# Attention block of a small audio tower: four maxima products a unit in place of six, in a new order

## Chip, cores and metric

The kernel runs on one core of one Trainium2 chip. The metric is the device time of one execution in microseconds (us). The kernel before takes 1871.29 us, the median of 3 runs from 1869.54 to 1872.24.

## What is computed

Three blocks run one after another over 128 batches: a tokenizer (4-token windows with a small softmax), attention, and a routed feed-forward block. Only the attention is touched. Per batch, of 128 rows and 192 features:

```python
# 8 heads of 24 features; thirds q3,q4,q5 / k3,k4,k5 / v3,v4,v5 of 8 features each
x3 = attn(q4, concat(k3, k4), concat(v3, v4))
x4 = attn(q5, concat(k3, k5), concat(v3, v5))
x5 = attn(q5, concat(k4, k5), concat(v4, v5))
h = h + concat(x3, x4, x5) @ w_proj.T + b_proj
```

`attn` is softmax(q k^T / sqrt(24)) v. Each query row's maximum over its keys is subtracted before the exponential, so every head needs the query-key products twice: once for the maxima, and once for the scores with the maximum folded in.

## The kernel before

**Stage and bodies.** `attend` (from L453) runs as a software pipeline, one batch a body. The loop holds four bodies a round, 30 rounds (bodies 3 to 122), and the bodies before and after are written out. Body i computes the scores of batch i, while other steps work on batches up to four ahead or three behind. A body has four units (u = 0 to 3) on TensorE; a unit has two heads a, b of batch i to score, and two heads c, d whose maxima it takes, of batch i + 1 for u = 0, 1 and of batch i + 2 for u = 2, 3. The four heads lie in four different row groups of 32 rows of the array, so products of different heads can run side by side, while two products of one head share rows.

**A unit on TensorE** (`products`, from L571). Six score products of 256 columns (L583) fill three PSUM banks: p_s1 with head b, p_s0 with head a, p_s5 with a and then b. Six maxima products (L587) fill p_maxa, which has two banks, and p_maxb, which has one. Where two row groups write one bank, the second waits on a semaphore that the first sets at its end: `pe_half` for p_s5 and `pe_fc` for p_maxa's second bank (blocks 4 and 5, 128 columns each from c and from d). Other waits at the unit's products: `dve_ma`, `dve_mb` (VectorE has read p_maxa, p_maxb of the unit before), `act_e1`, `act_e5`, `act_e0` (ScalarE has read the score banks). In unit 2 the first maxima product also waits for the transposes of the batch's keys and queries, `dma_k` and `dma_q`.

**Between the units** stand on TensorE: probabilities times values (L658, 24 products a body), the products of q, k, v of batch i + 3 right behind unit 2 (`qkv`, L627 to L633, into p_z), the transposes of the outputs (L669), and the projection right behind unit 3.

**The other engines.** ScalarE takes three exponentials a unit (L701, L704, L707), copies p_z to `raw` (L725) and `vn` (L726) once qkv is done, and `ot` (L716). VectorE reduces p_maxa (L749) and p_maxb (L751) in each unit; behind unit 1 it makes the minima of the negated maxima and writes them to `qk` (L766 to L768), and it has a few steps more (L757, L774, L777, L784). GpSimd splits `raw` into high and low halves: the keys at L802 and L805 (which sets `pool_k`), the queries at L808 and L811 (`pool_q`), L813 (`pool_q5`); and it does so for x and for the attention's output.

**The SP queue** issues five DMA transposes a body, in this order: xt (L535), kt (L540, waits for `pool_k`), qt (L545, waits for `pool_q`, `pe_ma[1]`, `pe_mb[1]`), yt (L550), qm (L556, waits for `dve_min`, `pool_q5`, `pe_s0[3]`). Keys and queries that body i transposes are of batch i + 2, and so unit 2 of the same body is their first user. Each wait is `ready`: a wait and an increment, with the count computed from the loop's register where it isn't one that a register holds already.

Of the kernel before, what the change touches and what calls it, by code (L numbers as in the profile page):

```python
# [15 lines left out]
NP = 127  # L16
# [434 lines left out]
def attend(nc, t, NB):  # L451

    with ExitStack() as ctx:  # L453
# [69 lines left out]
        def _(sp):  # L523

            def ready(signal, count):

                sp.wait_ge(signal, count)
                sp.sem_inc(sp_ready, 1)

            def body(i, r):  # L530
# [5 lines left out]
                if within(i + 2, NB):  # L536
                    ready(pool_k, seen(i + 3))
                    if within(i - 2, NB):
                        ready(pe_s0[3], seen(i - 1))
                    sp.dma_start_transpose(kt[:, (r + 2) % U].rearrange("p k g n -> p (k g) n"), qk[:, r % 2, K0:K0 + 768]).then_inc(dma_k, 16)  # L540
                    ready(pool_q, seen(i + 3))
                    if within(i, NB):
                        ready(pe_ma[1], seen(i + 1))
                        ready(pe_mb[1], seen(i + 1))
                    sp.dma_start_transpose(qt[:, r % 2].rearrange("p k g n -> p (k g) n"), qk[:, r % 2, 0:512]).then_inc(dma_q, 16)  # L545
# [24 lines left out]
        def _(pe):  # L570
# [3 lines left out]
            def products(i, r, u):  # L574
# [15 lines left out]
                if has_s:  # L590
                    if u == 0:
                        pe.wait_ge(dma_qm, seen(16 * (i + 1)))
                    pe.wait_ge(act_e1[u - 1] if u else act_e1[3], seen(i + 1 if u else i))
                    score(p_s[1][:, 0:2, :], b, 0, slice(0, 2))
                if has_m:
                    if u == 2:
                        pe.wait_ge(dma_k, seen(16 * (bm + 1)))
                        pe.wait_ge(dma_q, seen(16 * (bm + 1)))
                    pe.wait_ge(dve_ma[u - 1], seen(i + 2 if u < 3 else i + 3))
                    maximum(p_ma[:, 4:5, :], c, 1, slice(2, 3)).then_inc(pe_fc[u], 1)  # L600
# [3 lines left out]
                if has_m:  # L604
                    maximum(p_ma[:, 0:2, :], d, 0, slice(0, 2))
                if has_s:
                    score(p_s[1][:, 2:4, :], b, 1, slice(0, 3, 2)).then_inc(pe_s1[u], 1)
                if has_m:
                    maximum(p_ma[:, 2:4, :], d, 1, slice(0, 2))
                    pe.wait_ge(pe_fc[u], seen(bm + 1))  # L610
                    maximum(p_ma[:, 5:6, :], d, 1, slice(2, 3)).then_inc(pe_ma[u], 1)
                    pe.wait_ge(dve_mb[u - 1], seen(i + 2 if u < 3 else i + 3))
                    maximum(p_mb[:, 0:2, :], c, 0, slice(0, 2))
# [3 lines left out]
                if has_m:  # L617
                    maximum(p_mb[:, 2:4, :], c, 1, slice(0, 2)).then_inc(pe_mb[u], 1)
                if has_s:
                    pe.wait_ge(pe_half[u], seen(2 * i + 1))  # L620
                    score(p_s5[:, 2:4, :], b, 2, slice(1, 3)).then_inc(pe_half[u], 1)
                    score(p_s[0][:, 2:4, :], a, 1, slice(0, 3, 2)).then_inc(pe_s0[u], 1)
# [110 lines left out]
        def _(dve):  # L733
# [10 lines left out]
            def maxima(i, r, u):  # L744
                bm, pair = (i + 1, 2 + (1 - u)) if u < 2 else (i + 2, 1 - (u - 2))
                q = (r + 1) % 2 if u < 2 else r % 2
                if within(bm, NB):
                    dve.wait_ge(pe_ma[u], seen(bm + 1))
                    nc.vector.tensor_reduce(top[:, q, pair, 4:10], p_ma[:, 0:6, 0:NP], AX.X, ALU.max, negate=True).then_inc(dve_ma[u], 1)  # L749
# [3 lines left out]
            def body(i, r):  # L753
# [6 lines left out]
                if within(i + 1, NB):  # L760
                    dve.wait_ge(dve_mb[1], seen(i + 2))
                    got = top[:, (r + 1) % 2]
                    four = got[:, :, 0:8].rearrange("p a (e k) -> p a e k", e=2)
                    fifth = got[:, :, 8:10]
                    low = [slots((r + 1) % 2, 256 * x, HEADS)[:, :, 24].rearrange("p (a e) -> p a e", e=2) for x in range(3)]
                    nc.vector.tensor_tensor(low[0], four[:, :, :, 0], four[:, :, :, 1], ALU.min)  # L766
                    nc.vector.tensor_tensor(low[1], four[:, :, :, 2], fifth, ALU.min)
                    nc.vector.tensor_tensor(low[2], four[:, :, :, 3], fifth, ALU.min).then_inc(dve_min, 1)  # L768
# [442 lines left out]
```

## Time and profile before

| | |
|---|---|
| median of 3 runs | 1871.29 us |
| profiled execution, its own time | 1873.42 us |
| its span in the profile | 1871.7 us |
| tokenizer, about | 0 to 320 us of the span |
| attention | about 370 to 1400 us |
| feed-forward, about | 1450 to 1871 us |
| TensorE busy, whole span | 1789.6 us, 96% |
| VectorE, ScalarE, GpSimd busy | 1495.4, 1462.8, 1252.7 us |

The profile is of one execution. Busy times are sums of the instructions' spans; on TensorE products overlap and their ends are modelled, so that a busy TensorE need not be at its peak. Of a row group's work only starts can be compared exactly.

### The profile page before, as it was taken

Reading aid. Unit: us, or ns where it says so; the run is one execution under the profiler, and the core shown is the slowest. Engines: PE = TensorE matmul, PEld = TensorE weight load, DVE = VectorE, ACT = ScalarE, POOL = GpSimd, SP = SyncE. Lnnn points to the kernel's source line nnn. Section 1 sums busy time; section 2 is a strip of 40 time slices with the busy share of each in tenths; the row PEclk is TensorE's granted clock in tenths of the full one; section 3 lists DMA queues with packets and bytes.
Section 4 is the critical chain, followed back from the end, with each engine's and each line's share of the span. In section 5 each row is a group of like instructions: output and inputs, shape, how many; then the busy total and the mean of one; then the engine's idle time right before and its main releaser. Section 6 shows DMA issues by size and latency. Waiting matters only on the chain. (4 is left out here: it accounts for less than half of the span.)

```text
span 1871.7 us, 59000 instructions
## 1 busy us (share of the span) xinstructions
PE 1789.6 (96%) x20032; PEld 1015.8 (54%) x20032; DVE 1495.4 (80%) x3674; ACT 1462.8 (78%) x2983; POOL 1252.7 (67%) x2306
## 2 busy tenths in 40 slices
PE   5999999599999999999999999999994999999999
PEld 3677777244444444444444444444442777777776
DVE  6887878689999999999999999999994555555554
ACT  4666666288889888988898889988884777777775
POOL 4777776467777777777777777777753565666661
PEclk9999999699999999999999999999997999999999
DMA  7344442144444444444444444444441333333332
GB/s 192 90 112 112 112 112 68 35 81 87 89 88 89 89 88 88 90 88 90 88 88 88 90 89 89 87 92 88 88 79 28 72 70 68 70 67 71 65 74 54
DMA packets 503935, 159.49 MB, mean 85 GB/s; under 512 B 452176, under 2 KB 503120, under 8 KB 503888
## 3 DMA queue, kind: packets, MB, share of 16 engines
q1 hardware_dynamic: 503888, 158.90, 40.0%
q8 instruction: 26, 0.43, 0.1%
q14 instruction: 21, 0.17, 0.0%
HBM read 37.26 MB, written 12.48 MB: 27 GB/s over the span
## 5 line engine op out<-in xcount | busy, mean ns | idle before, releaser
L749 DVE TENSOR_REDUCE tops<-p_maxa 128x6 f32<-128x762 f32 x512 | 482.4, 942 | 63.2 <-PE p_maxa L587 61.4
L658 PE MATMUL p_o<-probs,vn 127*32 127x256 f32 x6144 | 410.8, 385 | 0.3 <-DVE att L777 0.3
L583 PE MATMUL p_s<-qm,kt 32*128 32x256 f16 x3072 | 399.9, 276 | 1.0 <-ACT probs L704 0.4
L701 ACT ACTIVATE probs<-p_s 128x512 f32<-128x512 f32 x512 | 305.4, 596 | 108.9 <-PE p_s L583 95.1
L751 DVE TENSOR_REDUCE tops<-p_maxb 128x4 f32<-128x508 f32 x512 | 345.9, 676 | 0.0
L707 ACT ACTIVATE probs<-p_s 128x512 f32<-128x512 f32 x512 | 309.0, 603 | 0.0
L704 ACT ACTIVATE probs<-p_s 128x512 f32<-128x512 f32 x512 | 304.6, 595 | 0.3 <-PE p_s L583 0.2
L587 PE MATMUL p_maxa<-kt,qt 24*128 24x256 f16 (+1 forms) x2048 | 283.9, 250 | 17.4 <-DMA qt<-qk 8.8
L1056 DVE TENSOR_TENSOR gel_lo<-gel,gel_hi 128x512 f16<-128x512 f32 x192 | 151.0, 787 | 168.9 <-ACT gel_hi L1028 168.7
L802 POOL TENSOR_TENSOR qk<-raw,one 128x384 f16<-128x384 f32 x128 | 105.7, 826 | 220.8 <-ACT raw L725 220.8
L583 PEld LDWEIGHTS p_s<-qm,kt 32*128 32x128 f16 x3072 | 135.2, 91 | 182.6 <-issue 164.8
L658 PEld LDWEIGHTS p_o<-probs,vn 127*32 127x32 f32 x6144 | 160.6, 109 | 131.4 <-issue 48.8
L1020 ACT ACTIVATE gel<-f_w,b 128x512 f32<-128x512 f32 x192 | 131.9, 687 | 117.4 <-PE f_w L969 117.3
L587 PE MATMUL p_maxb<-kt,qt 24*128 24x256 f16 x1024 | 200.5, 275 | 0.1
L980 PE MATMUL f_y<-w_hi,gel_hi 128*128 128x192 f16 x768 | 188.8, 246 | 0.2 <-DVE gel_lo L1056 0.2
L982 PE MATMUL f_y<-w_hi,gel_lo 128*128 128x192 f16 x768 | 188.9, 246 | 0.0
L981 PE MATMUL f_y<-w_lo,gel_hi 128*128 128x192 f16 x768 | 188.9, 246 | 0.0
L1126 POOL TENSOR_TENSOR f_hx<-f_hn,f_one 128x192 f16<-128x192 f32 x120 | 85.3, 711 | 154.0 <-ACT f_hn L1007 146.9
L587 PEld LDWEIGHTS p_maxa<-kt,qt 24*128 24x128 f16 x2048 | 109.1, 91 | 139.9 <-PE p_maxa L587 108.0
L208 ACT ACTIVATE tanhs<-pa 128x384 f32<-128x384 f32 x128 | 62.7, 490 | 99.8 <-PE pa L154 99.8
L1028 ACT ACTIVATE gel_hi<-gel 128x512 f16<-128x512 f32 x192 | 120.9, 630 | 7.1
L396 POOL TENSOR_TENSOR diag<-ident,weight 128x256 f32<-128x256 f32 x128 | 79.2, 620 | 54.2 <-DVE weight L296 45.0
(213 smaller groups left out, 4556.9 us busy)
## 6 DMA issues: line engine op xcount, KB each, us to landing
xt_a<-in_xt SPq DMA_DIRECT2D x32, 512.0 KB, 4.4
xt_b<-in_xt SPq DMA_DIRECT2D x64, 256.0 KB, 5.2
out<-out_sb SPq DMA_DIRECT2D x32, 336.0 KB, 2.6
xt<-hx SPq DMA_TRANSPOSE x128, 2.4
kt<-qk SPq DMA_TRANSPOSE x128, 2.8
qt<-qk SPq DMA_TRANSPOSE x128, 2.4
qm<-qk SPq DMA_TRANSPOSE x128, 2.7
yt<-ay SPq DMA_TRANSPOSE x128, 2.3
```

Of the source, the lines that this page charges most:

```text
L583: return nc.tensor.matmul(o, kt[full(j), r, kind, g, :], qm[full(j), r % 2, versions, g, :], start=True, stop=True, skip_group_check=True)
L587: return nc.tensor.matmul(o, qt[short(j), rq, kind, gm, :], kt[short(j), rk, cols, gm, :], start=True, stop=True, skip_group_check=True)
L658: last = nc.tensor.matmul(p_o[32 * j:32 * j + 32, blocks, :], vn[0:NP, r, src:src + 32], probs[0:NP, r % 2, QUAD * g + j, kind * 256:(kind ...
L701: nc.scalar.activation(probs[:, r % 2, h + 1, 0:512], p_s[1][:, :, :].rearrange("p x n -> p (x n)"), ACT.Exp, scale=SCALE).then_inc(act_e1 ...
L704: nc.scalar.activation(probs[:, r % 2, h:h + 2, 512:768], p_s5[:, :, :].rearrange("p (h x) n -> p h (x n)", h=2), ACT.Exp, scale=SCALE).th ...
L707: nc.scalar.activation(probs[:, r % 2, h, 0:512], p_s[0][:, :, :].rearrange("p x n -> p (x n)"), ACT.Exp, scale=SCALE).then_inc(act_e0[u], 1)
L749: nc.vector.tensor_reduce(top[:, q, pair, 4:10], p_ma[:, 0:6, 0:NP], AX.X, ALU.max, negate=True).then_inc(dve_ma[u], 1)
L751: nc.vector.tensor_reduce(top[:, q, pair, 0:4], p_mb[:, :, 0:NP], AX.X, ALU.max, negate=True).then_inc(dve_mb[u], 1)
L980: nc.tensor.matmul(o, ghi[:, c % 3, n], t.w2_hi[:, c, :], start=False, stop=False)
L981: nc.tensor.matmul(o, ghi[:, c % 3, n], t.w2_lo[:, c, :], start=False, stop=False)
L982: last = nc.tensor.matmul(o, glo[:, c % 3, n], t.w2_hi[:, c, :], start=False, stop=(c == HCH - 1))
L1056: nc.vector.tensor_tensor(glo[:, c % 3, :], gel[:, c % 2, :], ghi[:, c % 3, :], ALU.subtract).then_inc(dve_lo[c], 1)
```

## The change

The maxima of block k5 and of k3, k4 against q5 (kind 1) now come from one product of 384 columns for each of the heads c and d, each into a bank of p_maxa of its own. The two products of kind 0 share p_maxb, c first, d behind a wait on `pe_fc` at the unit's end. `pe_ma` counts to two a unit, so that its waiters (SP before qt, VectorE before the first reduction) wait for 2(n + 1) in place of n + 1. The reduction of p_maxa reads 2 x 3 blocks of 127, as many elements as before, and two minima instructions stand for three.

```diff
@@ SP queue, between kt and qt
                     if within(i, NB):
-                        ready(pe_ma[1], seen(i + 1))
+                        ready(pe_ma[1], seen(2 * (i + 1)))
                         ready(pe_mb[1], seen(i + 1))
@@ products(i, r, u)
                 if has_m:
-                    if u == 2:
-                        pe.wait_ge(dma_k, seen(16 * (bm + 1)))
-                        pe.wait_ge(dma_q, seen(16 * (bm + 1)))
                     pe.wait_ge(dve_ma[u - 1], seen(i + 2 if u < 3 else i + 3))
-                    maximum(p_ma[:, 4:5, :], c, 1, slice(2, 3)).then_inc(pe_fc[u], 1)
+                    maximum(p_ma[:, 0:3, :], c, 1, slice(0, 3)).then_inc(pe_ma[u], 1)
+                    maximum(p_ma[:, 4:7, :], d, 1, slice(0, 3)).then_inc(pe_ma[u], 1)
                 if has_s:
                     pe.wait_ge(act_e5[u - 1] if u else act_e5[3], seen(i + 1 if u else i))
                     score(p_s5[:, 0:2, :], a, 2, slice(1, 3)).then_inc(pe_half[u], 1)
-                if has_m:
-                    maximum(p_ma[:, 0:2, :], d, 0, slice(0, 2))
                 if has_s:
                     score(p_s[1][:, 2:4, :], b, 1, slice(0, 3, 2)).then_inc(pe_s1[u], 1)
                 if has_m:
-                    maximum(p_ma[:, 2:4, :], d, 1, slice(0, 2))
-                    pe.wait_ge(pe_fc[u], seen(bm + 1))
-                    maximum(p_ma[:, 5:6, :], d, 1, slice(2, 3)).then_inc(pe_ma[u], 1)
                     pe.wait_ge(dve_mb[u - 1], seen(i + 2 if u < 3 else i + 3))
-                    maximum(p_mb[:, 0:2, :], c, 0, slice(0, 2))
+                    maximum(p_mb[:, 0:2, :], c, 0, slice(0, 2)).then_inc(pe_fc[u], 1)
                 if has_s:
                     pe.wait_ge(act_e0[u - 1] if u else act_e0[3], seen(i + 1 if u else i))
                     score(p_s[0][:, 0:2, :], a, 0, slice(0, 2))
-                if has_m:
-                    maximum(p_mb[:, 2:4, :], c, 1, slice(0, 2)).then_inc(pe_mb[u], 1)
+                    score(p_s[0][:, 2:4, :], a, 1, slice(0, 3, 2)).then_inc(pe_s0[u], 1)
                 if has_s:
                     pe.wait_ge(pe_half[u], seen(2 * i + 1))
                     score(p_s5[:, 2:4, :], b, 2, slice(1, 3)).then_inc(pe_half[u], 1)
-                    score(p_s[0][:, 2:4, :], a, 1, slice(0, 3, 2)).then_inc(pe_s0[u], 1)
+                if has_m:
+                    pe.wait_ge(pe_fc[u], seen(bm + 1))
+                    maximum(p_mb[:, 2:4, :], d, 0, slice(0, 2)).then_inc(pe_mb[u], 1)
@@ VectorE, body
-                    nc.vector.tensor_tensor(low[0], four[:, :, :, 0], four[:, :, :, 1], ALU.min)
-                    nc.vector.tensor_tensor(low[1], four[:, :, :, 2], fifth, ALU.min)
-                    nc.vector.tensor_tensor(low[2], four[:, :, :, 3], fifth, ALU.min).then_inc(dve_min, 1)
+                    nc.vector.tensor_tensor(low[:, 0], fourth[:, :, :, 0], fourth[:, :, :, 1], ALU.min)
+                    nc.vector.tensor_tensor(low[:, 1:3], fifth[:, 0:2], fifth[:, 2:3].broadcast_to([128, 2, QUAD, 2]), ALU.min).then_inc(dve_min, 1)
```

The waits on `dma_k` and `dma_q` are still taken in unit 2 in front of the first maxima product.

TensorE, unit 2 of the loop's third body, before (p_s1, p_s5, p_s0 are score banks; what stands behind the unit is qkv):

```order
L583 MATMUL p_s1<-qm,kt 128x256 [waits act_e11]
L587 MATMUL p_maxa<-kt,qt 128x128 [waits dve_ma1,dma_q,dma_k]
L583 MATMUL p_s5<-qm,kt 128x256 [waits act_e51]
L587 MATMUL p_maxa<-kt,qt 128x256
L583 MATMUL p_s1<-qm,kt 128x256
L587 MATMUL p_maxa<-kt,qt 128x256
L587 MATMUL p_maxa<-kt,qt 128x128 [waits pe_fc2]
L587 MATMUL p_maxb<-kt,qt 128x256 [waits dve_mb1]
L583 MATMUL p_s0<-qm,kt 128x256 [waits act_e01]
L587 MATMUL p_maxb<-kt,qt 128x256
L583 MATMUL p_s5<-qm,kt 128x256 [waits pe_half2]
L583 MATMUL p_s0<-qm,kt 128x256
```

The same unit of the changed kernel:

```order
L583 MATMUL p_s1<-qm,kt 128x256 [waits act_e11]
L587 MATMUL p_maxa<-kt,qt 128x384 [waits dve_ma1,dma_q,dma_k]
L587 MATMUL p_maxa<-kt,qt 128x384
L583 MATMUL p_s5<-qm,kt 128x256 [waits act_e51]
L583 MATMUL p_s1<-qm,kt 128x256
L587 MATMUL p_maxb<-kt,qt 128x256 [waits dve_mb1]
L583 MATMUL p_s0<-qm,kt 128x256 [waits act_e01]
L583 MATMUL p_s0<-qm,kt 128x256
L583 MATMUL p_s5<-qm,kt 128x256 [waits pe_half2]
L587 MATMUL p_maxb<-kt,qt 128x256 [waits pe_fc2]
```

The wait on `pe_fc` stood at the seventh of twelve products and stands at the last of ten; the product that it waits for was the second of the unit, of 128 columns, and is now the sixth, of 256.

The SP queue in the loop's second body, as a difference (the third and fourth body change alike):

```order
 L535 DMA_TRANSPOSE xt<-hx 128x3x128 [waits pool_x,pe_qkv]
 L540 DMA_TRANSPOSE kt<-qk 128x6x128 [waits pool_k,pe_s03]
-L545 DMA_TRANSPOSE qt<-qk 128x4x128 [waits pool_q,pe_ma1,pe_mb1]
+L527 REGISTER_ALU [waits pool_q]
+L545 DMA_TRANSPOSE qt<-qk 128x4x128 [waits pe_ma1,pe_mb1]
 L550 DMA_TRANSPOSE yt<-ay 128x3x128 [waits pool_y,pe_proj]
```

The new count needs a register instruction between kt and qt. The loop's first body had one there before the change, and has now an instruction that updates several registers in its place.

## Rows read from the trace of the kernel before

**Rows 1.** Busy times by stretch; PEclk is the granted share of TensorE's clock:

```profile
400.00:1400.00 1000.00, 995.54 (x13509) 459.12 (x13505) 934.28 (x1841) 895.65 (x1840) 730.16 (x1456) 1.00 0.45 88
```

**Rows 2.** Who waited for whom, 600 to 1300 us (86 bodies): us, times, longest:

```profile
POOL qk L802 <- ACT raw L725: 138.9, 87, 1.9
...
PEld p_maxa L587 <- PE p_maxa L587: 73.2, 346, 0.2
```

**Rows 3.** Timeline, unit 2 of a second body: start us, duration us, engine, line:

```profile
800.36 0.21 PE L587 MATMUL p_maxa<-kt,qt 24*128 24x128 f16 x1
...
800.37 0.28 PE L587 MATMUL p_maxa<-kt,qt 24*128 24x256 f16 x1
...
800.49 0.37 PE L587 MATMUL p_maxa<-kt,qt 24*128 24x256 f16 x2
...
800.63 0.09 PEld L587 LDWEIGHTS p_maxa<-kt,qt 24*128 24x128 f16 x1 [0.15 <-PE p_maxa L587]
...
800.70 0.10 PEld L583 LDWEIGHTS p_s<-qm,kt 32*128 32x128 f16 x2
...
800.76 0.27 PE L583 MATMUL p_s<-qm,kt 32*128 32x256 f16 x1
...
800.96 0.39 PE L627 MATMUL p_z<-wqkv_ahi,xt 128*128 128x512 f16 x1
```

**Rows 4.** Timeline, from that unit's products to unit 2 one body on:

```profile
802.25 0.44 ACT L725 ACTIVATE raw<-p_z 128x320 f32<-128x320 f32 x1
...
803.66 0.55 POOL L805 TENSOR_TENSOR qk<-raw,qk 128x192 f16<-128x192 f32 x1
...
804.38 1.21 SPq L540 DMA_TRANSPOSE kt<-qk  x1
...
805.84 1.19 SPq L545 DMA_TRANSPOSE qt<-qk  x1
...
808.28 0.28 PE L583 MATMUL p_s<-qm,kt 32*128 32x256 f16 x1
808.33 0.21 PE L587 MATMUL p_maxa<-kt,qt 24*128 24x128 f16 x1
...
808.99 0.39 PE L627 MATMUL p_z<-wqkv_ahi,xt 128*128 128x512 f16 x1
```

**Rows 5.** Timeline of the SP queue, a fourth body's end and a first body:

```profile
813.88 1.19 SPq L545 DMA_TRANSPOSE qt<-qk  x1
...
819.19 1.19 SPq L535 DMA_TRANSPOSE xt<-hx  x1
820.63 1.21 SPq L540 DMA_TRANSPOSE kt<-qk  x1
822.15 1.19 SPq L545 DMA_TRANSPOSE qt<-qk  x1
```

**Rows 6.** Timeline of TensorE, unit 2 of a fourth and of a first body:

```profile
816.39 0.21 PE L587 MATMUL p_maxa<-kt,qt 24*128 24x128 f16 x1
...
817.02 0.39 PE L627 MATMUL p_z<-wqkv_ahi,xt 128*128 128x512 f16 x1
...
824.65 0.21 PE L587 MATMUL p_maxa<-kt,qt 24*128 24x128 f16 x1
```

**Rows 7.** Groups by line and shape, 600 to 1300 us: count, busy us, mean ns:

```profile
L587 PE MATMUL p_maxb<-kt,qt 24*128 24x256 f16 x691 | 133.9, 273 | 0.0
```

**Rows 8.** Timeline, weight load and product of unit 0 in the body between:

```profile
804.75 0.23 PE L587 MATMUL p_maxa<-kt,qt 24*128 24x128 f16 x1
...
805.09 0.09 PEld L587 LDWEIGHTS p_maxa<-kt,qt 24*128 24x128 f16 x1 [0.23 <-PE p_maxa L587]
```

**Rows 9.** Timeline of VectorE, unit 0 and the last of the minima there:

```profile
805.35 0.95 DVE L749 TENSOR_REDUCE tops<-p_maxa 128x6 f32<-128x762 f32 x1 [0.36 <-PE p_maxa L587]
...
809.18 0.18 DVE L768 TENSOR_TENSOR qk<-tops 128x8 f16<-128x8 f32 x1
```

**Rows 10.** Timeline of GpSimd in that first body:

```profile
819.73 0.55 POOL L805 TENSOR_TENSOR qk<-raw,qk 128x192 f16<-128x192 f32 x1
```

More of the change, by code:

```diff
@@ L594, in products @@
                     score(p_s[1][:, 0:2, :], b, 0, slice(0, 2))
+                if has_m and u == 2:
+                    pe.wait_ge(dma_k, seen(16 * (bm + 1)))
+                    pe.wait_ge(dma_q, seen(16 * (bm + 1)))
                 if has_m:
-                    if u == 2:
-                        pe.wait_ge(dma_k, seen(16 * (bm + 1)))
-                        pe.wait_ge(dma_q, seen(16 * (bm + 1)))
                     pe.wait_ge(dve_ma[u - 1], seen(i + 2 if u < 3 else i + 3))
-                    maximum(p_ma[:, 4:5, :], c, 1, slice(2, 3)).then_inc(pe_fc[u], 1)
+                    maximum(p_ma[:, 0:3, :], c, 1, slice(0, 3)).then_inc(pe_ma[u], 1)
+                    maximum(p_ma[:, 4:7, :], d, 1, slice(0, 3)).then_inc(pe_ma[u], 1)
                 if has_s:
@@ L747, in maxima @@
                 if within(bm, NB):
-                    dve.wait_ge(pe_ma[u], seen(bm + 1))
-                    nc.vector.tensor_reduce(top[:, q, pair, 4:10], p_ma[:, 0:6, 0:NP], AX.X, ALU.max, negate=True).then_inc(dve_ma[u], 1)
+                    dve.wait_ge(pe_ma[u], seen(2 * (bm + 1)))
+                    nc.vector.tensor_reduce(top[:, q, pair, 4:10].rearrange("p (e k) -> p e k", e=2),
+                                            p_ma[:, :, :].rearrange("p (e k) n -> p e k n", e=2)[:, :, 0:3, 0:NP],
+                                            AX.X, ALU.max, negate=True).then_inc(dve_ma[u], 1)
                     dve.wait_ge(pe_mb[u], seen(bm + 1))
@@ L762, in body @@
                     got = top[:, (r + 1) % 2]
-                    four = got[:, :, 0:8].rearrange("p a (e k) -> p a e k", e=2)
-                    fifth = got[:, :, 8:10]
-                    low = [slots((r + 1) % 2, 256 * x, HEADS)[:, :, 24].rearrange("p (a e) -> p a e", e=2) for x in range(3)]
-                    nc.vector.tensor_tensor(low[0], four[:, :, :, 0], four[:, :, :, 1], ALU.min)
-                    nc.vector.tensor_tensor(low[1], four[:, :, :, 2], fifth, ALU.min)
-                    nc.vector.tensor_tensor(low[2], four[:, :, :, 3], fifth, ALU.min).then_inc(dve_min, 1)
+                    fourth = got[:, :, 0:4].rearrange("p a (e k) -> p a e k", e=2)
+                    fifth = got[:, :, 4:10].rearrange("p a (e k) -> p k a e", e=2)
+                    low = slots((r + 1) % 2, 0, NQ)[:, :, 24].rearrange("p (x a e) -> p x a e", x=3, e=2)
+                    nc.vector.tensor_tensor(low[:, 0], fourth[:, :, :, 0], fourth[:, :, :, 1], ALU.min)
+                    nc.vector.tensor_tensor(low[:, 1:3], fifth[:, 0:2], fifth[:, 2:3].broadcast_to([128, 2, QUAD, 2]), ALU.min).then_inc(dve_min, 1)
                 maxima(i, r, 2)
```

## Prediction

> **What bounds the kernel now.** I read the busy times by stretch first. From 400 to 1400 us TensorE is busy for 995.54 of 1000 us, VectorE for 934.28, ScalarE for 895.65, and the granted clock is 1.00, the 2.4 GHz level [rows 1]. So TensorE looks like the bound, and two products fewer a unit look like a gain. But its spans overlap, so this share cannot tell whether a unit may end sooner. The waits add two things: GpSimd's L802 waits for ScalarE's `raw` in every body, and TensorE waits 0.21 us (73.2 over 346) for a product of its own in every unit, which is the wait on `pe_fc` [rows 2].
>
> The timeline then shows a loop through five engines that closes once a body:
> - Unit 2's first maxima product starts at 800.36, qkv at 800.96: 0.60 us [rows 3].
> - `raw` starts at 802.25: 1.29 us after qkv. L805, which sets `pool_k`, ends at 804.21, kt is issued at 804.38, qt at 805.84 [rows 4].
> - The next unit 2's first maxima product starts at 808.33, 2.49 us after qt [rows 4]. In the fourth body it is 2.51 us (813.88 to 816.39), in the next first body 2.50 us (822.15 to 824.65) [rows 5, 6].
>
> The last is the sign: behind the issue of qt this product comes at the same distance in every body, whenever the unit began. In the body of 808.28 the unit's first score product is only 0.05 us ahead [rows 4], so TensorE's own work is just covered there. The kernel is bound by the latency of this loop, with TensorE close behind. From the second body's product (800.36) to the fourth's (816.39) are two turns, 8.02 us each; to the next first body's (824.65) it is 8.26 us. On the mean a body lasts 8.1 us (691 p_maxb products, 8 a body, in 700 us [rows 7]).
>
> **Unit 2, from its first maxima product to qkv.** Before, this is 0.60 us in the second body (and in the first, which waits for qt alike), 0.66 in the third (808.33 to 808.99) and 0.63 in the fourth (816.39 to 817.02) [rows 3, 4, 6]. After the change a chain of three links decides it, since the unit's last product waits for the sixth:
> - Two products of one head follow each other at 0.12 us if the first has 256 columns (800.37 to 800.49) [rows 3]. A 128-column product lasts 0.23 us in unit 0 [rows 8] and a 256-column one 0.28 [rows 3], so 128 columns more are 0.05 us: 384 columns take 0.17 us, and then c's p_maxb product can start.
> - Its end must be seen. No row has this for a maxima product of 256 columns. The nearest two: from 128 columns at 800.36 to the load that waits for them at 800.63, 0.27 us; from the score product of 256 columns on p_s5, issued with the maxima at 800.36, to the load that waits for it at 800.70, 0.34 us [rows 3]. The second has the same columns, and the first plus 0.05 us gives nearly it, so I take 0.34. The low end is 0.27. The high end is 0.39: in unit 0 the 128-column product starts at 804.75 and the load that waits for it at 805.09, 0.34 us [rows 8], and 0.05 us for the columns come on top.
> - From a unit's last product to what follows: 0.20 us (800.76 to 800.96) [rows 3].
>
> Sum: 0.17 + 0.34 + 0.20 = 0.71 us. That is 0.11, 0.05, 0.08 and 0.11 us more in the second, third, fourth and first body: **+0.35 us a round** of four. Of this VectorE takes no share: its first reduction waits 0.36 us for TensorE in unit 0 [rows 9], and both 384-column products are done some 0.2 us sooner than the last p_maxa product was. So p_maxb is free for unit 2 earlier than before.
>
> Here the Trainium skill has a rule that speaks for the change. It says that each matmul carries about 60 cycles of overhead on trn2, whatever its columns ("TensorEngine Tiling (Array Packing)", Instruction Overhead). By it two products fewer would take some 0.05 us off a unit at 2.4 GHz, my estimate from its figure, and unit 2 would come to 0.66 us. The trace does not bear it out on this path: products of different heads start within 0.01 us of each other (800.36 and 800.37) [rows 3].
>
> **The SP queue.** Between kt and qt a register instruction is added in the second, third and fourth body. The first body had one before, and there kt to qt is 1.52 us (820.63 to 822.15) [rows 5] against 1.46 (804.38 to 805.84) [rows 4]. I take 0.07 us: three times that is **+0.21 us a round**. The first body's own exchange I cost at nothing; its bounds are 0 and 0.03. Nothing hides this term, since qt's issue is a link of the loop. The ends are 0 and 0.10 for each body.
>
> **The minima and what they release.** VectorE's work in units 0 and 1 moves ahead by about 0.2 us, and one of the minima goes. So `dve_min` comes 0.3 us or more sooner (the last of the minima ended at 809.36 [rows 9]), qm and xt are issued sooner, and the queue is free earlier for kt. This pays only where kt waits for the queue and not for GpSimd. In the second body L805 ends at 804.21 and kt comes 0.17 us later [rows 4]. In the first body L805 ends at 820.28 and kt comes 0.35 us later, at 820.63, with xt just ahead of it (819.19 plus 1.44) [rows 5, 10]. Of this 0.35 the usual 0.17 and 0.07 for the register instruction stay: **-0.11 us a round**. Bounds: 0, and -0.18.
>
> **Units 0, 1 and 3** are off the loop. They come to 0.71 us by the same three links where they were 0.67, and unit 1, which waits for VectorE, gets a little shorter. Cover for this is the wait for qt, which grows to 0.1 to 0.3 us in every body because the loop gets longer than TensorE's own work. If that cover is gone, three units by 0.04 us come on top, 0.1 us a body. The new waits of VectorE on two counts cost nothing, as the second product starts with the first. Tokenizer and feed-forward are untouched.
>
> **Sum.** 0.35 + 0.21 - 0.11 = 0.45 us a round, times 30 rounds = 13.5 us. Some 8 bodies outside the loop have no register instructions: 0.09 us each, 0.7 us. Together +14.2 us. Against the profiled execution's own 1873.42 us this gives 1887.6. The median of the runs lies 2.1 us lower, so the forecast is **1885.5 us**.
>
> **Rivals.**
> 1. *The completion wait is covered* and unit 2 gets shorter: if c's p_maxb product is over when the others are done, unit 2 takes 0.17 + 0.12 + 0.20 = 0.49 us, 0.53 us a round less than before in place of 0.35 more. With SP's +0.21 and -0.11 it is -0.43 a round: 1858 us. It decides when the wait costs under about 0.23 us. For it: the wait has moved from the middle of the unit to its end. Against it: only three score products stand between, and the two measured waits are 0.27 and 0.34. Chance 0.07. In this case the kernel is faster.
> 2. *The number of products decides.* If TensorE's own work were the bound and each product had a cost of its own in it, 8 fewer a body would show. Two products in a row on one row group stand 0.12 us apart, where 256 columns at 2.4 GHz take 0.107: 0.013 us each, times 8 and 128 is 13 us, 1858 us. For it: TensorE's 99.6%. Against it: the constant 2.50 us behind qt. By the overhead rule of the Trainium skill ("TensorEngine Tiling (Array Packing)", Instruction Overhead) it would be 26 us, an estimate. Chance 0.03.
> 3. *Unit 2 stays as long as it was*, since the first part of the wait is absorbed, and only SP's terms are left: +0.10 us a round, 3 us, 1874.3 us. This takes a wait of 0.25 us, close to the 128-column row. Chance 0.10.
> 4. *TensorE's own work becomes the bound*, if the three links cost more in units 0, 1 and 3 than worked out, say 0.80 in place of 0.71 us in each unit: 0.09 by four is 0.36 us a body, of which about 0.2 is covered. 0.16 by 126 is 20 us on top: about 1905 us. Chance 0.05.
>
> **Numbers.** The forecast's case has 0.75. Its own range, from the bounds: with 0.27 for the wait in all four bodies it is 8.4 us less, 1877; with 0.39 for the wait and 0.10 for each of SP's instructions it is 8.7 us more, 1894. The full range has to hold 8 in 10 and reaches from 1873, which takes in rival 3, to 1896. Two measurements of this kernel can tell 0.2% (3.7 us) from no change. Faster: rivals 1 and 2, 0.10. Same: most of rival 3, 0.10. Slower: 0.80.
>
> **What the profile after would show.** Unit 2 from its first maxima product to qkv: 0.71 us in all four bodies. Its first maxima product still 2.50 us behind qt's issue, and at least 0.1 us behind the unit's first score product in every body. kt to qt 1.52 or 1.53 us in all four bodies. kt in the first body 0.24 us behind L805's end. VectorE's idle time before L746 smaller in unit 0, and TensorE's wait for its own product kept, now at the load for p_maxb. A body of 8.22 us. I am wrong if unit 2 takes under 0.65 us, or if the distance from qt's issue to the first maxima product varies.

## The result, and the profile after

The changed kernel takes 1893.81 us (median of 4 runs, 1891.67 to 1896.09), the kernel before 1870.41 us beside it (1869.08 to 1872.24): a ratio of 1.0125, 95% interval 1.0107 to 1.0142. It is slower by 23.4 us, where 14.2 us were forecast. The profiled execution took 1896.09 us, with a span of 1894.4 us.

Busy times of the changed kernel in the same stretch as [rows 1]; the columns are TensorE, weight loads, VectorE, ScalarE, GpSimd, then the granted clock:

```profile
400.00:1400.00 1000.00, 997.49 (x12255) 511.24 (x12256) 905.70 (x1682) 875.25 (x1803) 720.08 (x1440) 1.00 0.44 87
```

TensorE's share rose from 99.6% to 99.7%, the clock is still at its 2.4 GHz level, and VectorE, ScalarE and GpSimd are all less busy: their work is spread over longer bodies. The weight loads alone show more, 511.24 us for 459.12, though there are 1249 fewer of them; fewer of them overlap. Next the waits from 600 to 1300 us, against [rows 2]:

```profile
POOL qk L800 <- ACT raw L722: 153.3, 85, 2.0
...
PEld p_s L583 <- PE p_s L583: 51.9, 233, 0.2
...
PEld p_maxb L587 <- DVE tops L750: 13.2, 84, 0.2
```

GpSimd waits for `raw` 1.80 us a body, where it was 1.60. TensorE's wait for a product of its own moved, but not to where I put it: it is not the load for p_maxb but a load for p_s, the one that waits for `pe_half`. The last row, 0.16 us a body, is unit 1's wait for VectorE. The groups of the same stretch (count, busy us, mean ns), against [rows 7]:

```profile
L587 PE MATMUL p_maxb<-kt,qt 24*128 24x256 f16 x677 | 185.2, 274 | 0.0
L587 PE MATMUL p_maxa<-kt,qt 24*128 24x384 f16 x676 | 113.4, 330 | 0.0
```

677 products at 8 a body are 84.6 bodies in 700 us, 8.27 us each; before there were 86.4, 8.10 us each. The 384-column product lasts 0.33 us by the profile's modelled ends, 0.056 more than one of 256 columns (0.05 was estimated).

The timeline of unit 2 in a second body (start us, us; compare [rows 3]):

```profile
808.13 0.34 PE L587 MATMUL p_maxa<-kt,qt 24*128 24x384 f16 x2
808.14 0.10 PEld L583 LDWEIGHTS p_s<-qm,kt 32*128 32x128 f16 x2
808.14 0.39 PE L583 MATMUL p_s<-qm,kt 32*128 32x256 f16 x3
...
808.29 0.27 PE L587 MATMUL p_maxb<-kt,qt 24*128 24x256 f16 x1
...
808.58 0.09 PEld L583 LDWEIGHTS p_s<-qm,kt 32*128 32x128 f16 x1 [0.22 <-PE p_s L583]
808.64 0.09 PEld L587 LDWEIGHTS p_maxb<-kt,qt 24*128 24x128 f16 x1
...
808.86 0.39 PE L624 MATMUL p_z<-wqkv_ahi,xt 128*128 128x512 f16 x1
```

From the first maxima product to qkv it is now 0.73 us (0.60 before). a's p_s5 product starts with the 384-column ones at 808.14, and b's load, which waits for it, comes at 808.58: 0.44 us, where the same wait took 0.34 in [rows 3]. The unit's last product, d's on p_maxb, follows that load by 0.06 us.

The loop, from that unit on (compare [rows 4]):

```profile
810.15 0.44 ACT L722 ACTIVATE raw<-p_z 128x320 f32<-128x320 f32 x1
...
811.57 0.55 POOL L803 TENSOR_TENSOR qk<-raw,qk 128x192 f16<-128x192 f32 x1
812.28 1.22 SPq L540 DMA_TRANSPOSE kt<-qk  x1
813.83 1.19 SPq L545 DMA_TRANSPOSE qt<-qk  x1
...
816.28 0.28 PE L583 MATMUL p_s<-qm,kt 32*128 32x256 f16 x1
816.33 0.34 PE L587 MATMUL p_maxa<-kt,qt 24*128 24x384 f16 x2
...
817.05 0.39 PE L624 MATMUL p_z<-wqkv_ahi,xt 128*128 128x512 f16 x1
```

And the SP queue in the fourth and the first body that follow (compare [rows 5]):

```profile
820.48 1.21 SPq L540 DMA_TRANSPOSE kt<-qk  x1
822.07 1.19 SPq L545 DMA_TRANSPOSE qt<-qk  x1
...
828.79 1.21 SPq L540 DMA_TRANSPOSE kt<-qk  x1
830.36 1.19 SPq L545 DMA_TRANSPOSE qt<-qk  x1
```

The 2.50 us from qt to the first maxima product stand as before (813.83 to 816.33). kt to qt is 1.55, 1.59 and 1.57 us here, where it was 1.46 and, in the first body, 1.52.

**The loop added up.** All links taken singly over 600 to 1300 us, mean of a body in us. "kt late" runs from the end of GpSimd's second k operation (L805, now L803) to kt's issue, "unit 2" from its first maxima product to qkv. The links left out are raw to GpSimd's second k operation (1.44, up to 1.46 in e11), that operation itself (0.55) and qkv to raw (1.31). "Cover" is how far the first maxima product stands behind the unit's first score product: where it is 0.00 to 0.01 in a body, TensorE's own work holds that body.

| version | kt late | kt to qt | qt to unit 2 | unit 2 | cover | body | x126, against before | measured, ratio |
|---|---|---|---|---|---|---|---|---|
| before | 0.207 | 1.477 | 2.507 | 0.622 | 0.167 | 8.113 | | |
| the change | 0.180 | 1.558 | 2.508 | 0.728 | 0.132 | 8.276 | +20.5 | 1.0125 |
| e1_sp_count | 0.180 | 1.478 | 2.518 | 0.734 | 0.064 | 8.213 | +12.6 | 1.0083 |
| e2_before_count2 | 0.180 | 1.556 | 2.508 | 0.598 | 0.220 | 8.142 | +3.7 | 1.0019 |
| e3_p5_first | 0.179 | 1.568 | 2.505 | 0.697 | 0.150 | 8.253 | +17.6 | 1.0100 |
| e8_p5_first_count | 0.179 | 1.478 | 2.512 | 0.705 | 0.072 | 8.175 | +7.8 | 1.0066 |
| e4_repeat_unit2 | 0.180 | 1.559 | 2.507 | 0.835 | 0.131 | 8.381 | +33.8 | 1.0198 |
| e5_repeat_unit0 | 0.228 | 1.558 | 2.506 | 0.746 | 0.144 | 8.342 | +28.9 | 1.0166 |
| e10_after_unit2_only | 0.234 | 1.477 | 2.508 | 0.793 | 0.203 | 8.318 | +25.8 | 1.0130 |
| e9_after_units013 | 0.178 | 1.558 | 2.506 | 0.604 | 0.135 | 8.155 | +5.3 | 1.0035 |
| e11_after_unit1_only | 0.179 | 1.477 | 2.579 | 0.664 | 0.008 | 8.220 | +13.5 | 1.0048 |
| e12_mixed | 0.179 | 1.478 | 2.517 | 0.633 | 0.068 | 8.120 | +0.9 | 1.0017 |

The links add up to the body, to within 0.002 us for the kernel before and the change. Times 126, the bodies give the measured differences to within 5 us (e8: 7.8 by the bodies, 12.4 by the ratio; e11: 13.5 and 9.0). So the change's 23.4 us are, a round of four bodies: unit 2 +0.42, kt to qt +0.32, kt late -0.11, the rest +0.02, together 0.65 us, or 20.5 us over 126 bodies. The other 3 us come at the stage's end: in the profiled execution the last qkv but two starts 19.3 us later than before (1388.01 against 1368.75), the last one 23.4 us later (1408.97 against 1385.58). So the last two bodies take 10.0 and 11.0 us here, where e4, the change with one product more, has 9.0 and 8.5. No run tells the cause. One kt and one qt there took 2.62 and 1.76 us of the queue, where they take 1.2 elsewhere:

```profile
1391.44 2.62 SPq L540 DMA_TRANSPOSE kt<-qk  x1
1394.31 1.76 SPq L545 DMA_TRANSPOSE qt<-qk  x1
```

### The profile page after: what moved, and what is told of

Same layout as the page of the kernel before. It is cut to its first block and busy times, and to the rows that moved or that the text cites. A ratio compares the mean times of both kernels' runs of the same rounds, so it can differ in the third digit from the quotient of the medians.

```text
span 1894.4 us, 56914 instructions
## 1 busy us (share of the span) xinstructions
PE 1812.3 (96%) x19008; PEld 1078.8 (57%) x19008; DVE 1487.7 (79%) x3546; ACT 1460.4 (77%) x2983; POOL 1251.4 (66%) x2306
## 5 line engine op out<-in xcount | busy, mean ns | idle before, releaser
L583 PEld LDWEIGHTS p_s<-qm,kt 32*128 32x128 f16 x3072 | 164.7, 92 | 268.5 <-issue 177.8
L587 PE MATMUL p_maxb<-kt,qt 24*128 24x256 f16 x1024 | 282.9, 276 | 0.8
L655 PEld LDWEIGHTS p_o<-probs,vn 127*32 127x32 f32 x6144 | 160.6, 109 | 117.1 <-issue 20.5
L587 PE MATMUL p_maxa<-kt,qt 24*128 24x384 f16 x1024 | 173.6, 333 | 16.9 <-DMA qt<-qk 9.2
L587 PEld LDWEIGHTS p_maxb<-kt,qt 24*128 24x128 f16 x1024 | 93.5, 91 | 33.5 <-DVE tops L750 21.7
```

The lines of the kernel that those rows point to most:

```text
L583: return nc.tensor.matmul(o, kt[full(j), r, kind, g, :], qm[full(j), r % 2, versions, g, :], start=True, stop=True, skip_group_check=True)
L587: return nc.tensor.matmul(o, qt[short(j), rq, kind, gm, :], kt[short(j), rk, cols, gm, :], start=True, stop=True, skip_group_check=True)
L655: last = nc.tensor.matmul(p_o[32 * j:32 * j + 32, blocks, :], vn[0:NP, r, src:src + 32], probs[0:NP, r % 2, QUAD * g + j, kind * 256:(kind ...
```

## The experiments

Each was timed in five rounds against the kernel before.

**1. SP waits for VectorE's count.** Since VectorE reads p_maxa only when both products have been counted, its `dve_ma[1]` stands for both, and needs no doubled value.

```diff
-ready(pe_ma[1], seen(2 * (i + 1)))
+ready(dve_ma[1], seen(i + 1))
```

> The changed kernel, with SP's wait on two increments of pe_ma[1] ahead of qt replaced by a wait on dve_ma[1] for i + 1 (VectorE has read that bank), a count that a register holds already. Theory L (the loop raw, pool_k, kt, qt, unit 2, qkv bounds the body): kt to qt falls from 1.54 to 1.59 us back to 1.46 in three bodies of a round and to 1.53 in the first, 0.3 us a round, 8 to 10 us in all: 1884 to 1886 us. Theory P (TensorE's own work bounds the changed kernel): SP's queue costs nothing, 1893 to 1895 us.

Measured: 1887.84 us, ratio 1.0083 [1.0070, 1.0097], 6 us off the change by the medians and 8 by the ratios; theory P had nothing, theory L 8 to 10. Its SP queue in a fourth and a first body:

```profile
816.22 1.22 SPq L540 DMA_TRANSPOSE kt<-qk  x1
817.68 1.19 SPq L545 DMA_TRANSPOSE qt<-qk  x1
...
824.44 1.21 SPq L540 DMA_TRANSPOSE kt<-qk  x1
825.97 1.19 SPq L545 DMA_TRANSPOSE qt<-qk  x1
```

1.46 and 1.53 us are back. The register work between the two transposes is a link of the loop and cost 0.08 us a body in the mean, where the prediction's 0.21 us a round are 0.05: 0.07 or 0.08 in the second and third body, 0.13 in the fourth, 0.04 in the first. Not all of the 10 us came back: the cover is 0.003 us in the third and fourth body, so that TensorE's own work holds these two, with 2.53 us from qt to unit 2.

**2. The doubled count put into the kernel before.**

```diff
-ready(pe_ma[1], seen(i + 1))
+ready(pe_ma[1], seen(2 * (i + 1)))
...
-                    maximum(p_ma[:, 2:4, :], d, 1, slice(0, 2))
+                    maximum(p_ma[:, 2:4, :], d, 1, slice(0, 2)).then_inc(pe_ma[u], 1)
...
-                    dve.wait_ge(pe_ma[u], seen(bm + 1))
+                    dve.wait_ge(pe_ma[u], seen(2 * (bm + 1)))
```

> The kernel before with nothing changed but the count: pe_ma is also incremented by the product of blocks 2 and 3, so SP and VectorE wait for 2(n + 1). All products, their order and the minima stay. Theory L: kt to qt grows by 0.07 to 0.13 us in three bodies of a round, 0.2 to 0.33 us a round: 1876 to 1880 us. Theory P: 1870 to 1871 us, as before.

Measured: 1875.63 us, ratio 1.0019 [1.0009, 1.0028]. kt to qt grew by the same 0.079 us, 10 us over the kernel, but 6 of them came back. Two links shrank: kt late in the first body from 0.335 to 0.227, and unit 2 in the third and fourth body from 0.65 and 0.64 to 0.598, most likely since VectorE, which reads p_maxb of unit 1, had more time. So a delay at one link of this loop was not paid in full, because other links had been waiting for something outside it.

**3. One product repeated, in unit 2 and in unit 0.** The unit's last product is issued twice (the second version has `u == 0`).

```diff
+                    if u == 2:
+                        maximum(p_mb[:, 2:4, :], d, 0, slice(0, 2))
                     maximum(p_mb[:, 2:4, :], d, 0, slice(0, 2)).then_inc(pe_mb[u], 1)
```

> The changed kernel with the last product of unit 2 (d, kind 0, 256 columns) issued twice in a row, 0.12 us more of TensorE's work between the first maxima product and qkv. Theory L: the whole 0.12 us lies on the loop, 127 bodies, +15 us: 1908 to 1910 us. Theory P: +15 us too. The pair with the next run tells them apart.

> The changed kernel with the last product of unit 0 issued twice, the same 0.12 us of TensorE's work off the loop. Theory L: it is taken up by the wait for qt in unit 2, which was 0.13, 0.21, 0.05 and 0.12 us in the four bodies of a round; only the third body exceeds it, by 0.07 us a round: 1895 to 1898 us. Theory P: +15 us, 1908 to 1910 us.

Measured: unit 2 1.0198 [1.0184, 1.0212], 13.7 us over the change by the ratios; unit 0 1.0166 [1.0152, 1.0180], 7.7 us over it. The first is what the loop says: unit 2 is longer by 0.107 us a body, and all of it counts. By itself it can't tell the two theories apart, which both had 15 us for it. The second is not: unit 0 was to be covered (1895 to 1898 us were expected, 1903.25 measured), and more than half of its 0.11 us came through, although unit 1 took 0.07 us less behind it (0.740 for 0.812, as VectorE has read p_maxb by the time that the later unit needs it). The links tell how. The cover falls to 0.015 us in the third body, VectorE's reductions come later, and so do the minima, qm and xt on SP: kt late in the first body grows from 0.226 to 0.414 us. Unit 2 itself waits for VectorE in the third and fourth body (0.798 and 0.738). Units 0, 1 and 3 are off the loop, but not free. Nor does this pair tell the two theories apart: the four units together are 0.054 us a body longer than in the change, which is 6.8 us by theory P as well.

**4. a's p_s5 product ahead of the 384-column ones.**

```diff
+                if has_s:
+                    pe.wait_ge(act_e5[u - 1] if u else act_e5[3], seen(i + 1 if u else i))
+                    score(p_s5[:, 0:2, :], a, 2, slice(1, 3)).then_inc(pe_half[u], 1)
                 if has_m and u == 2:
...
                     maximum(p_ma[:, 4:7, :], d, 1, slice(0, 3)).then_inc(pe_ma[u], 1)
-                if has_s:
-                    pe.wait_ge(act_e5[u - 1] if u else act_e5[3], seen(i + 1 if u else i))
-                    score(p_s5[:, 0:2, :], a, 2, slice(1, 3)).then_inc(pe_half[u], 1)
```

> The change, with one thing moved: in each unit the score product of head a on p_s5 is issued ahead of the two 384-column maxima products and no longer behind them. In the changed kernel the load for b's product on p_s5, which waits for that product of a, comes 0.45 us behind its start, where the same wait took 0.34 us in the kernel before; the unit's last product comes 0.07 us behind it. Theory O (a product's completion is told in the order of issue, so 256 columns behind two products of 384 are told with these): the distance falls to 0.34 or 0.35 us, and the last product then waits for c's p_maxb product (0.18 + 0.34 = 0.51 us behind the first maxima product, where it was 0.53). A unit gets some 0.02 us shorter, and where the wait came from the score product even 0.05: 0.08 to 0.2 us a round in unit 2, so 2 to 6 us off 1893.8, 1888 to 1892. Rival D (the distance is 0.45 us because the product shares the array with three others, in whatever order they are issued): it stays 0.43 to 0.45 us, and the time within 0.1% of the change's.

> The same, and SP waits for VectorE's count in place of TensorE's doubled one, which takes the register instruction between kt and qt away in three of four bodies. That alone took 6 to 8 us off the change. If both links lie on the loop they add up: 1881 to 1886. If TensorE's own work is already the bound in the version with the other count (its bodies showed under 0.07 us between a unit's first score product and its first maxima product), only what the shorter units give counts: four units by 0.02 us are 0.08 us a body, 10 us, so 1877 to 1880. If neither counts any more, 1887 or 1888.

Measured: 1888.13 us, 1.0100 [1.0084, 1.0115], and with the other count 1881.24 us, 1.0066 [1.0052, 1.0079]. Unit 2 of the first of them:

```profile
812.12 0.34 PE L587 MATMUL p_maxa<-kt,qt 24*128 24x384 f16 x2
...
812.28 0.27 PE L587 MATMUL p_maxb<-kt,qt 24*128 24x256 f16 x1
...
812.60 0.28 PE L587 MATMUL p_maxb<-kt,qt 24*128 24x256 f16 x1
812.81 0.39 PE L624 MATMUL p_z<-wqkv_ahi,xt 128*128 128x512 f16 x1
```

In unit 0 b's p_s5 product came 0.346 us behind the unit's start, where it was 0.463, and the last product at 0.507, as theory O had it. In this kernel a product of 256 columns that is issued behind two of 384 is told with them, and rival D falls: beside the same other products the wait is 0.11 us shorter. Of the medians the move takes 5.7 us off the change, SP's count 6.0, both together 12.6: they add up, as links of one loop do. The last product now waits for c's p_maxb (812.28 to 812.60, 0.32 us): this is the chain that the prediction had, and it gives 0.69 us.

**5. qkv ahead of unit 2.** This opens the loop and leaves the work as it is. On ScalarE `raw` and `vn` stand between the two `exponentials` lines below. The diff is of the first version; in the second the removed count is `seen(i + 1)`.

```diff
+                    if within(i + 1, NB):
+                        ready(pe_mb[2], seen(i + 2))
...
-                    if within(i, NB):
-                        ready(pe_ma[1], seen(2 * (i + 1)))
-                        ready(pe_mb[1], seen(i + 1))
...
+                qkv(i)
                 products(i, r, 2)
-                qkv(i)
...
-                exponentials(i, r, 2)
...
+                exponentials(i, r, 2)
```

> The change, with qkv issued ahead of unit 2's products and not behind them, ScalarE's raw and vn copies ahead of unit 2's exponentials, and SP's waits between kt and qt replaced by one ahead of kt that has long been met. This opens the loop: raw no longer stands behind the landing of qt. Theory L (the loop is the bound and TensorE's own work close behind, about 8.16 us a body by the version with SP's other count): the body falls from 8.27 to 8.15 to 8.18 us and the time to 1878 to 1883; GpSimd's k pass no longer waits 0.26 us in the mean for raw. Rival T (TensorE's own work already sets 8.27 us): the time stays within 0.2% of 1893.8. Rival S: units 2 and 3 now follow each other without a pause, and ScalarE, with its two copies ahead of unit 2's exponentials, becomes late for p_s: TensorE's waits for L727 and its neighbours grow by over 0.1 us a body and the time goes over 1895.

> The same three moves in the kernel before. Theory L: the loop sets 8.11 us a body there, TensorE's own work 8.03 to 8.06 us (its first maxima product was 0.05 us behind the unit's first score product at the least); opened, the time falls from 1870.4 by 6 to 10 us, to 1860 to 1865. Rival T: TensorE's own work is the bound before as well, and nothing is gained: 1868 to 1872. Rival S: ScalarE is late in units 2 and 3, over 1875.

Measured: 1970.07 us, 1.0536 [1.0522, 1.0551], and 1971.02 us, 1.0531 [1.0516, 1.0545]. Both theories failed here: L had 1878 to 1883 and 1860 to 1865, T no change. It is rival S, and far larger than it was put. A body takes 8.95 to 8.97 us in both, whatever the products. Units 2 and 3 in the first of them:

```profile
801.49 0.44 ACT L720 ACTIVATE raw<-p_z 128x320 f32<-128x320 f32 x1 [0.66 <-PE p_z L629]
...
802.68 0.09 PEld L582 LDWEIGHTS p_s<-qm,kt 32*128 32x128 f16 x1 [0.26 <-ACT probs L697]
...
803.17 0.09 PEld L582 LDWEIGHTS p_s<-qm,kt 32*128 32x128 f16 x2 [0.29 <-ACT probs L700]
...
803.66 0.11 PEld L582 LDWEIGHTS p_s<-qm,kt 32*128 32x128 f16 x3 [0.19 <-ACT probs L703]
```

ScalarE waits 0.66 us for qkv, then unit 3 waits three times for ScalarE, 0.74 us together. In the kernel's own order qkv stands between units 2 and 3 and gives ScalarE that time. So what opens the loop costs more than the loop, and these two runs don't tell what the loop's removal alone would give.

**6. The change taken apart by unit.** In the first version unit 2 alone has the four products, in the second all units but 2, in the third unit 1 alone; the others issue the six products of before (the expectations say five by mistake). All three have the change's minima. SP waits as before in the first, for the doubled count in the second, for VectorE's count in the third. Maxima then land in other places of `tops` than the minima read, so the stabilizers are other ones.

```diff
+                if u == 2:
...
+                        maximum(p_ma[:, 4:5, :], c, 1, slice(2, 3)).then_inc(pe_fc[u], 1)
...
+                else:
...
-                    dve.wait_ge(pe_ma[u], seen(2 * (bm + 1)))
+                    if u == 2:
+                        dve.wait_ge(pe_ma[u], seen(bm + 1))
+                        nc.vector.tensor_reduce(top[:, q, pair, 4:10], p_ma[:, 0:6, 0:NP], AX.X, ALU.max, negate=True).then_inc(dve_ma[u], 1)
```

The condition shown is that of the second version; it is `u != 2` in the first and `u != 1` in the third.

> The kernel before, with the change's four products in unit 2 alone; units 0, 1 and 3 issue the five products of before, SP waits as before, the minima are the change's. (The maxima land in other places of tops than the minima read, so the stabilizers are wrong; the amount of work is the same.) Theory L (the loop through qt bounds the kernel): from its first maxima product to qkv unit 2 takes 0.72 or 0.73 us in place of 0.60 to 0.66, 0.41 us a round, less 0.08 to 0.11 for the first body, in which kt comes sooner: +9 to +11 us on 1870.4, so 1879 to 1882. Rival P (TensorE's own work bounds it): unit 2 is longer by 0.069 us a body in the mean, times 126 is 8.7 us, 1879; and the version with the other three units must then show more than this one.

> The change, with the five products of before in unit 2 alone; units 0, 1 and 3, the minima and SP's doubled count are the change's. (Stabilizers wrong, as in the version above.) Theory L: the loop has before's unit 2 and SP's term, 0.33 us a round less what the first body gives back, 3.5 to 7 us on 1870.4; TensorE's own work is longer by 0.068 - 0.046 + 0.070 = 0.09 us a body in these three units, where 0.05 us a body covers it: 1874 to 1878. Rival P: all of the 0.09 us counts, 11.6 us, 1882, and this version is slower than the one with the change in unit 2.

> The kernel before, with the change's four products in unit 1 alone (the one unit that they made shorter, 0.81 for 0.86 us), the minima of the change, and SP waiting for VectorE's count. (Stabilizers wrong again.) Theory L: unit 1 is off the loop, so its 0.05 us a body gives nothing; what is left is the first body's kt, up to 0.11 us a round, 0 to 3 us: 1867 to 1871. Rival P: 0.046 times 126 is 6 us more, 1861 to 1865, a kernel faster than before.

Measured: e10 1.0130 [1.0112, 1.0147], e9 1.0035 [1.0025, 1.0045], e11 1.0048 [1.0035, 1.0061]. Unit 2 alone carries as much as the whole change, the other units and SP's count together 6.5 us, so the parts do not add up to the whole. The order of the two is theory L's. But e10 came out at 24 us, not 9 to 11, and e11 at 9, not 0 to 3. Unit 2 of e10, in a third body:

```profile
781.32 0.68 DVE L784 TENSOR_REDUCE tops<-p_maxb 128x4 f32<-128x508 f32 x1
...
781.75 0.34 PE L587 MATMUL p_maxa<-kt,qt 24*128 24x384 f16 x2
...
782.06 0.09 PEld L587 LDWEIGHTS p_maxb<-kt,qt 24*128 24x128 f16 x1 [0.21 <-DVE tops L784]
...
782.61 0.39 PE L654 MATMUL p_z<-wqkv_ahi,xt 128*128 128x512 f16 x1
```

c's p_maxb product waits for VectorE, whose reductions of units 0 and 1 start late with the six products, and with four products everything behind it is late too: 0.865 us from the first maxima product to qkv in the third and fourth body, 0.725 in the others. kt late in the first body is 0.439. In e11 the same wait sits in unit 1, which takes 1.07 us in place of the 0.81 of the change; the cover is 0.02 us in one body and 0.00 in the other three, and qkv follows qkv after 8.22 us in all four: TensorE's own work holds them. The pair e10 and e9 does not rule P out: unit 2 of e10 waits longer than either theory had it, and the measured lengths of the four units, taken as the only bound, give 22 and 9 us. What rules P out is SP's count alone (e1, e2) and e11, whose units are 0.27 us a body longer than before, 34 us by P, of which 9 count. So the change's early p_maxa in units 0 and 1 is worth something: it keeps VectorE ahead. The four products paid in neither version by themselves.

**7. A version from the readings.** The change's products in units 0, 1 and 3, in unit 2 five, with d's maxima as 384 and 256 columns, and SP on VectorE's count. The maxima's places in `tops` are laid out anew, so that the minima read the right ones.

```diff
+                if u == 2:
...
+                        maximum(p_ma[:, 0:1, :], c, 1, slice(2, 3)).then_inc(pe_fc[u], 1)
...
+                        maximum(p_ma[:, 4:7, :], d, 1, slice(0, 3)).then_inc(pe_ma[u], 1)
...
+                        pe.wait_ge(pe_fc[u], seen(bm + 1))
+                        maximum(p_ma[:, 1:3, :], d, 0, slice(0, 2)).then_inc(pe_ma[u], 1)
+                        pe.wait_ge(dve_mb[u - 1], seen(i + 2))
+                        maximum(p_mb[:, 0:2, :], c, 0, slice(0, 2))
...
+                        maximum(p_mb[:, 2:4, :], c, 1, slice(0, 2)).then_inc(pe_mb[u], 1)
```

> A version built from the readings: the change's four products in units 0, 1 and 3, five in unit 2 (128 columns of c first, then 384 and 256 of d, then c's two on p_mb, whose wait for one another is gone, so a score product ends the unit as in the kernel before), SP waiting for VectorE's count, the change's minima. tops has its places laid out anew, so that every maximum lands where the minima read it. Theory L, link by link: 0.60 us from the first maxima product to qkv, 1.46 from kt to qt (1.53 in the first body), 0.23 from L805's counterpart to kt in the first body: the loop would be 8.19, 8.08, 7.99 and 7.99 us; TensorE's own work holds the last two at 8.04 or so. Mean 8.09 against 8.11 before: 2 to 5 us off 1870.4, 1865 to 1869, the first version faster than both. Rival: VectorE becomes late, since unit 2's reduction of p_maxa starts later than with the four products, and a wait for p_maxb in unit 2 or 3 takes the gain: 1870 to 1876.

Measured: 1876.00 us beside 1872.50, 1.0017 [1.0008, 1.0026]. Not faster than before, where 1865 to 1869 us were expected, and not by the rival's way: TensorE's wait for VectorE's reading of p_maxb is 0.16 us a body, as in the change. The links of the loop came out as worked out in the first two bodies (8.21 and 8.08 us from `raw` to `raw`, for 8.19 and 8.08), but TensorE's own work holds the other two at 8.09 us, not at 8.04. A third body there:

```profile
774.74 0.28 PE L583 MATMUL p_s<-qm,kt 32*128 32x256 f16 x1
...
774.74 0.23 PE L587 MATMUL p_maxa<-kt,qt 24*128 24x128 f16 x1
...
775.41 0.39 PE L650 MATMUL p_z<-wqkv_ahi,xt 128*128 128x512 f16 x1
```

Score and maxima product start together: the cover is gone. My 8.04 was read off e9, as a third body's 8.087 us less its cover of 0.047. That leaves out that the second body's unit 2 had 0.216 us of cover there, behind which it took 0.597 us to qkv; without cover it takes 0.67, as here, and 8.04 becomes 8.11 at most. The sum over units says the same: units 0, 1 and 3 take 0.739, 0.812 and 0.743 us with the change's products and 0.671, 0.858 and 0.673 before, 0.09 us more a body, against covers of 0.058 and 0.070 us in the third and fourth body of the kernel before. The version takes, within 4 us, the time of the kernel before, with a shorter loop in some bodies and longer units: the two bounds lie that close together.

## Why the prediction was right, and where it fell short

The direction, the mechanism and the range held; the size, 14.2 us forecast and 23.4 measured, did not, and 1893.81 us lies just under the 1894 at which the forecast's own range ended. By its steps:

- **What bounds the kernel**: right. The 2.50 us behind qt stand, to within 0.02 us, in every body that has cover; where TensorE's own work holds a body it grows, to 2.53 us in e1 and to 2.64 in e11. SP's register work alone, which adds nothing to any computing engine, moves the time both ways (e1, e2), and a product more in unit 2 costs its whole length (e4).
- **Unit 2**: forecast 0.71 us in all four bodies, +0.35 us a round; measured 0.725 us, and 0.736 in the mean of the second bodies, +0.42. The size was nearly right, but the second link was the wrong one. The term "0.34 us until c's p_maxb product is seen" would have ended the unit at 0.69 if it had been 0.32, as e3 shows it (0.697 for the unit). What ended it was a's p_s5 product, which is told 0.45 us after its start because it was issued behind two products of 384 columns. The prediction took 0.34 us for a wait of 256 columns without asking what was issued just ahead of it. That the sum still came within 0.015 us is in part luck: 0.34 us was 0.02 too long for the wait that it named.
- **The SP queue**: forecast +0.21 us a round, measured +0.32, the larger miss. Each instruction was to cost 0.07 us and the first body nothing. The second and third cost 0.07 and 0.08; the fourth 0.13, since all of the queue's steps stand further apart in that stretch (0.076 to 0.093 us, against 0.065 to 0.071 in the third), and the first body's exchange 0.04, over its bound of 0.03.
- **The minima**: forecast -0.11 us a round, measured -0.11 (kt in the first body 0.335 us behind L805's end before, 0.226 after, 0.24 forecast). One part of its cause had not been seen. Before, the second of the three minima (L767) took 0.55 us in two of four bodies, when a GpSimd operation ran beside it; none of the change's two takes over 0.29.
- **Units 0, 1 and 3**: forecast as covered by 0.1 us at least. Measured 0.739, 0.812 and 0.743 us, not 0.71, and the cover in the third body was 0.05 us. It was nearly enough: e9, which has these three units, SP's count and the change's minima, is at +5.3 us by the bodies, e2, which has SP's count alone, at +3.7. But it gives no room.
- **Sum**: 0.45 us a round forecast, 0.65 measured; 0.07 of the difference is unit 2, 0.11 SP, the rest small parts. Over 31.5 rounds that is 20.5 us, and the last bodies of the stage add 3, for which the sum had no term.

Rival 1 and rival 3 fall with unit 2's length. Rival 2 falls too: with eight products fewer a body units 0, 2 and 3 got longer, and only unit 1 got shorter (0.812 for 0.858 us), where p_maxb waits less for VectorE. Here the overhead of about 60 cycles a matmul ("TensorEngine Tiling (Array Packing)" of the Trainium skill, Instruction Overhead) does not show, since products of different row groups start 0.003 us apart. The section's own example, that a product of 1 column takes as long as one of 60, fits a least length better than an addition to products of 256 columns. Rival 4 was near: with the SP term removed two bodies in four are held by TensorE's own work (e1, cover 0.003 us).

## What to carry to other kernels

Where a loop through several engines sets the pace, take the price of a change from the links alone, and sum them in every body of the round; then ask at once by how much the next bound (here TensorE, 0.05 us behind) covers the rest. In these runs a wait on a product lasted until the longer products issued ahead of it were done, so what other work waits for is better issued ahead of them (5.7 us here). A count that has to be computed in a register cost 0.07 to 0.13 us between two links; wait for a count that is already there if one tells the same.

## What the runs showed of the hardware

- **Completion in the order of issue.** The same product of 256 columns was seen after 0.34 us with one of 128 columns ahead of it, after 0.45 us with two of 384 ahead, and after 0.346 us once it was issued ahead of them. A product of 128 columns in the kernel before fits: 0.34 us in unit 0 [rows 8], where one of 256 columns was issued 0.004 us ahead of it, and 0.27 us in unit 2 [rows 3], where that one had started 0.24 us earlier. The Trainium skill says as much ("TensorE: Matmul & The Clock Gate", The mechanism: matmuls are monotone in start and end), and the times at which the waits were over agree. The starts don't: in unit 0 of the changed kernel a's product on p_s0, issued behind c's on p_maxb, starts at 0.129 us of the unit and c's at 0.176, as c's row group still has the 384 columns.
- **VectorE held up by GpSimd.** The second of the minima, with 16 elements, takes 0.22 us in the changed kernel and 0.60 us in e10, where it starts inside a GpSimd operation (start us, us):

```profile
798.55 0.20 DVE L799 TENSOR_TENSOR qk<-tops 128x8 f16<-128x8 f32 x1
798.61 0.55 POOL L859 TENSOR_TENSOR hx<-hn,hx 128x192 f16<-128x192 f32 x1
798.64 0.60 DVE L800 TENSOR_TENSOR qk<-tops 128x16 f16<-128x16 f32 x1
```

It ends at 799.24, just behind GpSimd's 799.16. The Trainium skill names a cause, a port pair that one of the two holds for a whole instruction when VectorE has two inputs in SBUF and GpSimd reads SBUF ("SBUF — State Buffer", SBUF: two separate sides), as here, and the trace agrees. The 0.38 us can matter through SP's queue, on which qm, xt and kt stand behind the minima; how much of e10's late kt is theirs no run tells.
